# A fused attention and routed feed-forward kernel: the last step's new state is started from the shared slot, and the hand-placed orders of the engines are set anew

## The reference

```
for _ in range(2):
    ctx = concat(integrated, v)
    x_shared, v_shared = inl(gelu(ctx @ w_s1 + b_s1) @ w_s2 + b_s2, integrated, v)
    x_r, v_r = the same with each token's two experts, weighted by their shares and added
    x_next = sw * x_shared + (1 - sw) * x_r          # v_next likewise
    halt = sigmoid(gelu(x_next @ w_h1 + b_h1) @ w_h2 + b_h2)
    refined = gelu(x_next @ w_f1 + b_f1) @ w_f2 + b_f2
    integrated = integrated + halt * refined * integration_weight
    v = v_next
# inl: v_next = sigmoid(a) * v - softplus(b) * (x - mu);  x_next = x + 0.1 * sigmoid(g) * v_next
```

## Time and profile before

| | us |
|---|---|
| median of 3 runs | 386.38 |
| runs | 386.26, 386.38, 389.85 |
| the profiled execution's own time | 388.05 |
| its span | 385.8 |
| PE busy | 342.6 (89%), 1663 instructions |
| DVE busy | 285.8 (74%), 620 instructions |
| ACT busy | 273.8 (71%), 444 instructions |
| POOL busy | 30.1 (8%) |
| mean granted clock of TensorE | 0.966 of full speed |

### The profile page before, as it was taken

The page is one execution under the profiler, slowest core; times in us unless marked ns, Lnnn a source line. Parts: engine busy times, 40 slices in busy tenths (PEclk is TensorE's granted clock), DMA queues, the critical chain, the costliest instruction groups (busy, mean ns, idle before and its releaser), DMA issues. The chain is left out here.

```text
span 385.8 us, 5578 instructions
## 1 busy us (share of the span) xinstructions
PE 342.6 (89%) x1663; PEld 220.3 (57%) x1663; DVE 285.8 (74%) x620; ACT 273.8 (71%) x444; POOL 30.1 (8%) x43
## 2 busy tenths in 40 slices
PE   4969699888988878997987998999999999999975
PEld 2435344434433356675564765776776786786743
DVE  7776966857624587589999897894995996798752
ACT  6642366586685789894958856896897997797812
POOL 9007731001000000000000000000000000000000
PEclk9976699999989999999999999999999999999988
DMA  4360000000000000000000000000000000001000
GB/s 117 92 168 3 3 1 5 0 1 6 3 3 0 1 3 2 1 0 2 1 0 1 2 0 2 1 0 0 3 0 0 3 0 27 3 0 29 1 28 27
DMA packets 10748, 5.15 MB, mean 13 GB/s; under 512 B 4355, under 2 KB 10655, under 8 KB 10719
## 3 DMA queue, kind: packets, MB, share of 16 engines
q1 hardware_dynamic: 10719, 4.81, 4.6%
HBM read 3.62 MB, written 1.05 MB: 12 GB/s over the span
## 5 line engine op out<-in xcount | busy, mean ns | idle before, releaser
L701 PE MATMUL bank<-qs,w_hi 128*128 128x512 f32 x160 | 65.6, 410 | 0.6 <-ACT qs L1017 0.5
L702 PE MATMUL bank<-qs,w_lo 128*128 128x512 f32 x160 | 62.4, 390 | 0.0
L884 ACT ACT_TABLE_LOAD x45 | 57.7, 1283 | 1.6 <-PEq L1393 0.7
L961 ACT ACTIVATE PT<-bank 77x512 f32<-77x512 f32 x64 | 35.3, 589 | 20.9 <-PE bank L812 14.1
L706 PE MATMUL bank<-KB,w_hi 128*128 128x512 f32 x160 | 42.8, 389 | 0.0
L1002 ACT ACTIVATE hid<-bank,cols 128x512 f32<-128x512 f32 (+1 forms) x48 | 31.4, 683 | 13.1 <-PE bank L668 12.5
L1281 DVE SCALAR_TENSOR_TENSOR masked<-Ib,cst,hid 128x512 f32<-128x512 bf16 x32 | 23.4, 751 | 20.9 <-ACT hid L1002 20.7
L701 PEld LDWEIGHTS bank<-qs,w_hi 128*128 128x128 f32 x160 | 30.1, 188 | 9.7 <-issue 2.0
L702 PEld LDWEIGHTS bank<-qs,w_lo 128*128 128x128 f32 x160 | 30.0, 188 | 7.7 <-issue 1.7
L706 PEld LDWEIGHTS bank<-KB,w_hi 128*128 128x128 f32 x160 | 30.0, 188 | 6.4
L823 PE MATMUL bank<-PT,VO 128*32 128x512 f32 x256 | 31.8, 598 | 0.4 <-ACT PT L961 0.4
(11 more groups left out here) (234 smaller groups left out, 662.2 us busy)
## 6 DMA issues: line engine op xcount, KB each, us to landing
x_tok<-in_x_dram SPq DMA_DIRECT2D x4, 256.0 KB, 3.4
out_dram<-x_tok SPq DMA_DIRECT2D x3, 256.0 KB, 2.3
hid<-in_L_ffn_expert_w_dram SPq DMA_DIRECT2D x1, 576.0 KB
masked<-in_L_ffn_expert_w_dram SPq DMA_DIRECT2D x2, 192.0 KB
wf_sb<-in_L_ffn_w_f_dram SPq DMA_DIRECT2D x2, 128.0 KB
qs<-mT SPq DMA_DIRECT2D x16, 8.0 KB
out_dram<-x_tok SPq DMA_DIRECT2D x2, 128.0 KB, 1.8
hid<-in_L_ffn_expert_w_dram SPq DMA_DIRECT2D x2, 96.0 KB
```

Of the source, the lines that this page charges most:

```text
L701: pe.matmul(t[:], lhsT=w2_hi[:, tile_of(k - 1, j), o:o + D], rhs=hi, start=(j == 0), stop=False)
L702: pe.matmul(t[:], lhsT=w2_lo[:, tile_of(k - 1, j), o:o + D], rhs=hi, start=False, stop=False)
L884: act.add_instruction(mybir.InstLoadActFuncSet(name=nc.get_next_instruction_name(), act_func_set_id=chosen, ins=[], outs=[]))
L961: step(act.activation(PT[0:KL, i % PT_TILES, :], ST[i % SCORE_BANKS][0:KL, :], ACT.Exp, scale=float(DH) ** -0.5))
```

## The change

**Arithmetic of the last step.** The part of xnext that is known before the experts is no longer made in `mix` 7 2 from the full sums, but in `mix` 7 0 from the shared slot's sums alone (the same four instructions). `mix` 7 1 now forms its slot's share of xnext by itself and adds it; it has 6 instructions in place of 5, `mix` 7 0 has 8 in place of 4, `mix` 7 2 has 8 in place of 12. DVE has one instruction more in all.

```diff
-        return (3, 4, 7)[k] if i < NB else (4, 5, 9 if i < LAST else 12)[k]
+        return (3, 4, 7)[k] if i < NB else (4, 5, 9)[k] if i < LAST else (8, 6, 8)[k]
...
                             step(dve.scalar_tensor_tensor(acc_a, alpha, 1.0, gate, ALU.add, ALU.mult))
+                        if s == LAST:
+                            known = acc_a
+                            settle()
+                            step(dve.tensor_tensor(acc_g, acc_g, nerr, ALU.mult))
+                            step(dve.tensor_tensor(acc_a, acc_a, vT[:, c, :], ALU.mult))
+                            settle()
+                            step(dve.scalar_tensor_tensor(known, acc_a, 0.5, acc_g, ALU.mult, ALU.add))
+                            settle()
+                            step(dve.scalar_tensor_tensor(known, known, DT / 2, xT[:, c, :], ALU.mult, ALU.add))
...
+                    elif (s, k) == (LAST, 1):
+
+                        v, known = vT[:, c, :], acc_a
+                        dve.wait_ge(act_done, act_at("sp", s, k))
+                        step(dve.scalar_tensor_tensor(beta, beta, 2.0, nerr, ALU.mult, ALU.mult))
+                        dve.wait_ge(act_done, act_at("gt", s, k))
+                        step(dve.scalar_tensor_tensor(alpha, alpha, 1.0, v, ALU.add, ALU.mult))
+                        settle()
+                        step(dve.tensor_tensor(alpha, alpha, beta, ALU.add))
+                        settle()
+                        step(dve.scalar_tensor_tensor(alpha, alpha, DT / 4, w, ALU.mult, ALU.mult))
+                        settle()
+                        step(dve.scalar_tensor_tensor(gate, gate, 1.0, alpha, ALU.add, ALU.mult))
+                        settle()
+                        step(dve.tensor_tensor(known, known, gate, ALU.add))
                     elif (s, k) == (LAST, 2):
...
-                        step(dve.tensor_tensor(acc_g, acc_g, nerr, ALU.mult))
-                        step(dve.tensor_tensor(acc_a, acc_a, vT[:, c, :], ALU.mult))
-                        settle()
-                        step(dve.scalar_tensor_tensor(known, acc_a, 0.5, acc_g, ALU.mult, ALU.add))
-                        settle()
-                        step(dve.scalar_tensor_tensor(known, known, DT / 2, xT[:, c, :], ALU.mult, ALU.add))
```

**Places.** LAST_FFN now holds places of all stages of the steps 6 and 7 that lie in the last stretch, and many places elsewhere have other numbers; of the tables a line or two:

```diff
-    0: 2, 1: 3, 2: 8, 3: 3, 4: 5, 5: 2, 6: 3, 7: 0,
+    0: 2, 1: 3, 2: 4, 3: 1, 4: 7, 5: 2, 6: 1, 7: 0,
...
-    0: 0, 1: 9, 2: 6, 3: 2, 4: 5,
+    0: 0, 1: 9, 2: 6, 3: 2, 4: 4,
...
-    0: 1, 1: 2, 2: 3, 3: 6, 4: 2, 5: 6, 6: 0, 7: 5,
+    0: 3, 1: 2, 2: 3, 3: 8, 4: 3, 5: 6, 6: 0, 7: 6,
```

More of the change, by code:

```diff
@@ L122 @@
     "norm": ((None, None, 13.57, None), 0), "o": ((18.51, None, 19.79, None), 0), "o2r": ((None, 24.14, None, None), 0),
[1 row of a table removed]
[L124 to L125 removed]
[1 row of a table added]
+    "lg": ((28.5, None, 32.95, None), 0), "lge": ((None, 32.7, None, None), 0), "vput": ((None, None, None, -4.42), 0),
+    "lgx": ((None, None, 30.88, None), 0), "bc": ((39.04, 37.12, None, None), 0.96),
 }
@@ L159 @@
 LAST_FFN = {
-    ("sp", 7, 2): (None, 202.72, None, None), ("gt", 7, 2): (None, 202.95, None, None), ("mix", 7, 2): (None, None, 198.08, None),
-    ("fin", 6, 0): (207.21, None, 209.54, None),
+    ("sp", 7, 2): (None, 202.72, None, None), ("gt", 7, 2): (None, 202.95, None, None), ("mix", 7, 2): (None, None, 197.78, None),
+    ("fin", 6, 0): (204.21, None, 207.62, None), ("halves", 7, 0): (None, 153.78, 145.62, None),
+    ("w1", 7, 0): (165.57, 162.69, None, None), ("mask", 7, 0): (None, None, 150.97, None),
@@ new lines @@
+    ("mask", 7, 1): (None, None, 157.18, None), ("round", 7, 2): (None, 173.75, None, None),
+    ("low", 7, 2): (None, None, 160.05, None), ("round", 7, 0): (None, 172.1, None, None),
+    ("low", 7, 0): (None, None, 164.75, None), ("round", 7, 1): (None, 187.67, None, None),
[5 rows of a table added]
+    ("mix", 7, 0): (None, None, 185.47, None), ("mix", 6, 1): (None, None, 159.87, None),
+    ("mix", 7, 1): (None, None, 185.49, None), ("mix", 6, 2): (None, None, 166.83, None),
+    ("tail", 6, 0): (184.78, 189.53, None, None), ("tail", 7, 0): (209.17, 215.22, None, None),
@@ L162 @@
+    ("tail", 6, 1): (202.3, 194.78, 186.26, None), ("tail", 7, 1): (219.24, 220.71, 212.19, None),
+    ("fin", 7, 0): (230.28, None, 220.66, None),
 }
 WARM_AT = {
-    0: -113.97, 1: -112.88, 2: -71.61, 3: -26.08, 4: -11.76, 5: 0.17, 6: -42.27, 7: 29.03,
+    0: -113.97, 1: -114.15, 2: -71.61, 3: -26.08, 4: -11.76, 5: 0.17, 6: -43.23, 7: 29.03,
 }
 WARM_PRODUCTS = {
-    0: 2, 1: 3, 2: 8, 3: 3, 4: 5, 5: 2, 6: 3, 7: 0,
+    0: 2, 1: 3, 2: 4, 3: 1, 4: 7, 5: 2, 6: 1, 7: 0,
 }
 HOLD_AT = {
-    0: 202.96, 1: 206.58, 2: 208.38, 3: 230.47, 4: 205.63,
+    0: 202.96, 1: 206.58, 2: 208.38, 3: 230.47, 4: 207.6,
@@ L184 @@
     ("mask", 1): {"dve": -17.09}, ("round", 2): {"act": 3.0}, ("low", 2): {"dve": -7.62}, ("round", 0): {"act": 6.35},
-    ("low", 0): {"dve": -1.56}, ("round", 1): {"act": -0.36}, ("low", 1): {"dve": 1.9}, ("w2", 0): {"pe": 9.55},
-    ("w2", 1): {"pe": 6.03}, ("w2", 2): {"pe": 8.37}, ("sp", 0): {"act": 0.78}, ("sp", 1): {"act": 11.17},
-    ("sp", 2): {"act": -1.5}, ("gt", 0): {"act": -5.57}, ("gt", 1): {"act": -1.49}, ("gt", 2): {"act": 1.76},
-    ("mix", 0): {"dve": 11.0}, ("mix", 1): {"dve": 0.12}, ("mix", 2): {"dve": -3.9}, ("tail", 0): {"pe": 0.87, "act": 1.75},
+    ("low", 0): {"dve": -5.11}, ("round", 1): {"act": -0.36}, ("low", 1): {"dve": 1.9}, ("w2", 0): {"pe": 9.55},
@@ L189 @@
+    ("w2", 1): {"pe": 6.03}, ("w2", 2): {"pe": 6.18}, ("sp", 0): {"act": 0.78}, ("sp", 1): {"act": 11.17},
+    ("sp", 2): {"act": -1.5}, ("gt", 0): {"act": -5.57}, ("gt", 1): {"act": -2.06}, ("gt", 2): {"act": 1.76},
+    ("mix", 0): {"dve": 11.0}, ("mix", 1): {"dve": 0.12}, ("mix", 2): {"dve": -2.28}, ("tail", 0): {"pe": 0.87, "act": 0.31},
     ("tail", 1): {"pe": 0.34, "act": 2.67, "dve": -1.07},
```

34 lines of the change are left out of this document (17 added, 17 removed), and 33 rows, old and new, of tables (BATCH_SHIFT, FFN_PLACES, LAST_FFN, PLACES).

## The result

The changed kernel takes 385.70 us (median of 20 runs, 385.28 to 387.77), the kernel before takes 388.62 us beside it (median of 20 runs, 386.26 to 391.36). The ratio is 0.9927, with an interval of 0.9908 to 0.9946: 2.9 us less, 0.73%. The forecast was 383.2 us in a range of 381.4 to 385.4, a difference of 3.15 us or 0.82%. So the difference was foretold nearly to size, and the time itself lies 0.3 us above the range.

The account below looks back on a forecast made before the run. PE's products bound the second iteration up to the last `w2`, then DVE's chain sets the end. Path 2.07 and clock 1.1 us, taken as 3.15 off the 386.38 us median, gave 383.2 us, range 381.4 to 385.4.

Parts of the forecast that it names:

- Part 1: Last step on DVE: four instructions move from `mix` 7 2 into idle time at `mix` 7 0; gate 2.65 us sooner.
- Part 2: ACT in the last step: `gt` 7 1 ahead of the gelus, later work about 1.1 us sooner; cover, not gain.
- Part 3: PE behind the last `w2`: fillers become the limit; first w_h1 products 1.3 us sooner, first w_f1 product 2.07 us sooner.
- Part 4: PE's tail: without the 0.90 and 0.81 us idle pieces the clock stays at 2.4 GHz; 1.1 us less, bounds 0 and 1.4.
- Part 5: Kernel start: fewer fillers gain nothing, as L1089 still ends at 43.4 us with POOL's instruction; bounds none or 2.65 us and more.
- the two rivals on the start: Start pays: 380.7 to 382.2 us, chance 0.15; start loses through PE at 1.2 GHz: up to 388.6 us, chance 0.03.
- Part 6: Middle: six more `keep` products and second-iteration exchanges on DVE and ACT cost nothing; at most 0.65 us for the products.
- The sign that the prediction named for a moved start or middle: A time of PE's first `w2` 7 2 product other than 356.77 us would show the forecast wrong.
- Sum: Whole kernel: 3.15 us taken off the runs' median of 386.38 us gives 383.2 us; as a span 382.6.
- the clock fell neither in the f1 groups nor in the h2 and f2 groups: Two tail rivals: clock falls in w_f1 groups, 384.3 us, chance 0.17; or later, up to 387.0 us, chance 0.05.
- The forecast's own case: Tail shortened by path and clock, start and middle giving nothing: 382.6 to 383.9 us, chance 0.5.
- the last rival: Tail not shortened, as DVE's chain in `mix` 7 0 and 7 1 overruns or a wait appears: 385 to 386.4 us, chance 0.1.

Follow-up runs that it names:

- hold_13: The changed kernel with thirteen fillers behind `fin` 6 in place of nineteen; 385.31 us (7 runs), ratio 0.9936 to the kernel before.
- before_hold_26: The kernel before with four more fillers behind the last step's second-layer products; 388.29 us against 388.87, ratio 0.9991.
- before_b: The kernel before, run again without any edit for another profiled execution; 388.87 us.
- hold_0: The changed kernel with all nineteen fillers ahead of the tail's first products removed; 388.5 us (12 runs), ratio 0.9988 to the kernel before.
- after_a: The changed kernel, run again without any edit for another profiled execution; 385.92 us.

## Why the prediction was right or wrong

**Part 1, the four instructions.** Right. `mix` 7 1 started behind them with no idle time, and the gate came 2.71 us sooner against the end of `w2`; 2.65 was predicted. Alpha needed no wait for ACT any more, and the gate's tanh left 0.87 us, where 0.9 was said.

**Part 2, ACT's order as cover.** Right for this change: put back, it makes the gate 0.13 us late and leaves h2 where it is. It would be wrong to read it as worth nothing anywhere, since without the new arithmetic the places move x_tok 1.0 us forward.

**Part 3, the fillers as the limit.** Right. h1 came 1.21 us sooner (1.3 predicted) and f1 2.09 (2.07), both against the end of `w2`. The fillers did set the start: with six fewer (`hold_13`) h1 comes 3.33 us behind `w2` in place of 4.62, so 1.29 of the 1.4 us that the prediction saw in DVE's hand were there. f1 gains only 0.58 of them, as it then waits for x_tok.

**Part 4, the clock.** Direction right, size somewhat high, and incomplete. From the start of f1 to h2 the profiled executions took 3.98 us before and 3.24 after: 0.74 where 1.1 was predicted. At full clock before's own groups take 3.08 (`before_hold_26`, `before_b`), so the fall cost 0.9 and PE's running ahead of ACT gave 0.16 back, not 1.4 and 0.3. The prediction gave as its reason that no idle piece over 0.3 us is left; pieces of 0.6 to 0.8 us ahead of f1 did no harm in four executions, and each fall came with about 0.9 us or more of idleness ahead of h1. What was missing is that this is no fixed cost: with the same idle pieces the clock did not fall in one execution, and stayed low for over 7 us in another. The Trainium skill says (TensorE: Matmul & The Clock Gate, "What's actually happening") that the throttled rate is the default and activity releases it; `hold_0` agrees, where without the fillers the clock was at half for 10.5 us.

**Part 5, the start.** Right, to a tenth of a microsecond: L1103 came sooner and ended with POOL's instruction at 43.3. The run with the start put back, 385.67 us, confirms that nothing came of it. So the two rivals on the start fell.

**Part 6, the middle.** Wrong by 0.4 us, inside its own bound. PE's waits at 154.42 and 158.56 us shrank from 1.58 and 0.54 to 1.13 and 0.32, as said, and no wait appeared up to 357 us. But `r1` 3, which the prediction saw delayed at no cost by the three fillers ahead of it, comes 0.38 us later against the product at 135 us, and the product at 154 us 0.37 us later; the term was put at nothing, with at most 0.65. No run took these fillers away, so that they are the cause is argued from the order. The exchanges in the second iteration did cost nothing: from 158 us to the end of the last `w2` every execution without half clock in between takes 206.4 to 206.5 us, with either places. The sign that the prediction named for a moved start or middle also came: the first `w2` 7 2 product is at 357.33, not 356.77. The traces give the steps: PE was 0.63 us ahead at 135 us, having had no half clock at 113; 0.26 ahead at 154; and behind once the clock fell from 176.5 to 180.5. That `w2` ends 0.58 us later is thus mostly the clock's doing, and within what unchanged kernels do.

**Sum.** This is the step that failed. The difference of 3.15 us was put on 386.38 us, the median of three runs. Those were 386.26, 386.38 and 389.85, and two of them come from the low end: of the 75 runs of the kernel before in the three comparisons 17 lie below 387, and the medians are 388.62, 388.74 and 388.87. (The prediction's terms, 2.07 and 1.1, add up to 3.17, not 3.15, which changes nothing.) From 388.62 the same sum gives 385.5, 0.2 us beside the measured 385.70. From the profiled execution's own 388.05, which was on the page, it gives 384.9, with the same bounds 383.1 to 387.1, and those hold the measured time. The sentence that put the profiled execution 1.67 us above the median took that as a property of the execution; it was one of the median. And the range held only the terms' bounds. Three runs that lie 3.6 us apart say that the base itself isn't known to a microsecond or two, and the range of 4 us had no room for that. That the measured difference, 2.92 us, comes so near to 3.15 is in part luck: the clock term and the middle each made the forecast 0.4 us too large, and what made up for most of it is the fall in before's tail, whose cost was read from one execution (0.9 us) and lies anywhere from 0 to 2.9.

**The rivals.** The tail was shortened, the clock fell neither in the f1 groups nor in the h2 and f2 groups in either execution of the changed kernel, the start neither paid nor lost. The forecast's own case held in its mechanism. The measured time lies in the band of the last rival (385 to 386.4 us, a tail that is not shortened), but that comes from the base: the tail is 2.9 us shorter. The change is within 1% of before, and so is the whole interval of the ratio; the prediction had put a chance of 0.27 on more than that.

## What to carry to other kernels

A predicted time is a base plus a difference, and the base needs its own bounds: where the few runs at hand scatter by more than the difference, put the difference on the execution whose trace was read, and widen the range by the scatter. When two edits shorten the same wait, cost them together (0.99 and 2.48 us alone were 2.71 together). Fillers ahead of a short last stage should end about when the real input is there: without them the clock fell, which cost more than the idle time itself, and each one too many delays the tail by its own 0.22 us until the next wait takes over. Here thirteen were enough and none too few; nothing between was run.

## What the runs showed of the hardware

The clock's falls are not a fixed property of a program. Three executions of one kernel with the same idle pieces (0.9 and 0.8 us) ahead of the tail stayed at 2.4 GHz, were at 1.2 GHz for about 4 us, and for about 7.5 us. Stretches of half clock ahead of the tail moved too: 113.5 to 117 us before, 114 to 118 and 145 to 149 in `before_b`, 176.5 to 180.5 after, 114.5 to 118.5 in `after_a`. This is seen beside run times that stand in groups, for the kernel before near 386.8, 388.7 and 389.8 us. The mean granted clock of the single runs goes with them: in the 56 runs of the kernel before that stand beside the experiments it is 0.975 or more in the 15 that took up to 387.1 us, 0.964 to 0.971 in the 18 from 388.0 to 389.1, and 0.966 or less in the rest. So the slower executions had, on the whole, more half clock; that each answers to one pattern of falls was not shown.

A DVE instruction on 128x4 values that takes 0.17 us alone took 2.65 us before and 3.49 after, and ended with POOL's 5 us instruction both times. In the fourteen profiled executions it starts anywhere from 38.10 to 41.27 us, takes 4.90 us where it comes first and 1.89 where it comes last, and ends 0.02 to 0.03 us behind POOL's each time. So it is held until POOL is done, and coming earlier only makes it longer. That POOL's instruction is what holds it rests on these ends; no run moved it.
